# Expert numbers as bytes instead of four-byte integers in a routed mixture-of-experts kernel

## The reference

```python
idx = jnp.argmax(router_probs, axis=-1)
onehot = jax.nn.one_hot(idx, E, dtype=xt.dtype)
...
h = jnp.einsum('te,td,edf->tf', onehot, xn, W1) + b1[idx]
h = jax.nn.relu(h)
y = jnp.einsum('te,tf,efd->td', onehot, h, W2) + b2[idx]
y = y * gates
```

## Time and profile before

| | |
|---|---|
| median of three runs | 201.38 us |
| the profiled execution's own time | 202.25 us |
| its span | 200.5 us |
| mean granted clock of TensorE | 0.91 |
| PE busy | 147.8 us, 74% |
| DVE busy | 161.1 us, 80% |
| ACT busy | 148.1 us, 74% |
| POOL busy | 114.3 us, 57% |

### The profile page before, as it was taken

One profiled execution on the slowest core, in us unless ns is written; L12 is line 12 of the kernel. 1 busy time (PEld: TensorE's weight loads), 2 busy tenths in 40 slices (PEclk: granted clock), 3 DMA queues, 4 the chain that ended last, 5 costly groups with the idle time before them and its releaser, 6 DMA issues.

```text
span 200.5 us, 5489 instructions
## 1 busy us (share of the span) xinstructions
PE 147.8 (74%) x1446; PEld 118.1 (59%) x1446; DVE 161.1 (80%) x819; ACT 148.1 (74%) x448; POOL 114.3 (57%) x200
## 2 busy tenths in 40 slices
PE   0068979988997795922369878998998997999400
PEld 0015736857566474821316767987888996888200
DVE  2455287999998869699698899999999999799900
ACT  2358979997975696527645887999999999898520
POOL 4323140508789765634469215768677687578650
PEclk9999999999999998585556999999999999999955
DMA  5997184000101101101342212223222222110000
GB/s 131 346 394 261 26 273 159 3 0 15 40 26 35 42 29 41 54 15 40 77 126 83 56 30 55 66 71 76 65 75 64 66 64 69 53 54 19 28 9 0
DMA packets 16415, 15.74 MB, mean 79 GB/s; under 512 B 2810, under 2 KB 13142, under 8 KB 16386
## 3 DMA queue, kind: packets, MB, share of 16 engines
q1 hardware_dynamic: 14034, 11.10, 19.0%
q0 software_dynamic: 2272, 4.27, 6.4%
q10 hardware_dynamic: 80, 0.03, 0.1%
HBM read 10.52 MB, written 5.33 MB: 79 GB/s over the span
## 4 chain that ended last, share of the span: by engine, by line
PE 43%; DVE 33%; issue 8%; ACT 6%; DMA 3%; ACTq 2%; POOLq 1%; SPq 1%; POOL 0%; DVEq 0%
PE bank L473 7%; DVE hl L1239 6%; PE bank L592 6%; PE bank L430 5%; PE bank L445 4%; DMA XN<-in_attn_embeddings 3%; DVE z L1248 3%; PE bank L502 3%; PE bank L580 3%; PE bank L576 2%; PE bank L578 2%; DVE zpart L1244 2%; PE bank L579 2%; PE bank L595 2%; DVE bn L1252 2%
## 5 line engine op out<-in xcount | busy, mean ns | idle before, releaser
L418 POOL DMA_INDIRECT out<-OUT,tok x39 | 40.5, 1039 | 26.5 <-issue 25.0
L383 POOL DMA_INDIRECT rows<-R,place x32 | 31.8, 994 | 18.0 <-DVE place L919 9.4
L592 PE MATMUL bank<-W2hl,hh 128*128 x156 | 32.6, 274 | 7.0 <-issue 3.2
L576 PE MATMUL bank<-sel,bias 96*128 96x128 bf16 x156 | 34.6, 222 | 0.0
L578 PE MATMUL bank<-xh,W1h 128*128 128x128 f16 x156 | 34.2, 219 | 0.0
L580 PE MATMUL bank<-xh,W1l 128*128 128x128 f16 x156 | 34.1, 218 | 0.0
L579 PE MATMUL bank<-xl,W1h 128*128 128x128 f16 x156 | 34.0, 218 | 0.0
L1239 DVE SCALAR_TENSOR_TENSOR hl<-bank,hh 128x512 f16<-128x512 f32 x39 | 26.9, 690 | 3.5 <-ACT hh L746 2.6
L595 PE MATMUL bank<-W2hl,hl 128*128 x156 | 27.9, 219 | 0.0
L746 ACT ACTIVATE hh<-bank 128x512 f16<-128x512 f32 x39 | 23.1, 593 | 6.1 <-PE bank L580 5.8
L359 POOL TENSOR_TENSOR rmag<-guarded,minus_half 128x4 f32<-128x4 f32 x8 | 8.2, 1022 | 27.0 <-ACT guarded L615 27.0
(11 more groups left out here) (197 smaller groups left out, 459.3 us busy)
## 6 DMA issues: line engine op xcount, KB each, us to landing
XR<-rows SPq DMA_DIRECT2D x39, 66.0 KB
W<-in_ffn_W SPq DMA_DIRECT2D x1, 2048.0 KB, 11.0
X<-in_attn_embeddings SPq DMA_DIRECT2D x2, 512.0 KB, 8.6
X<-in_attn_embeddings SPq DMA_DIRECT2D x1, 768.0 KB
out<-OUT,tok POOLq DMA_INDIRECT x39
rows<-padt SPq DMA_DIRECT2D x9, 66.0 KB
XN<-in_attn_embeddings SPq DMA_DIRECT2D x2, 256.0 KB, 7.9
rows<-R,place POOLq DMA_INDIRECT x32
```

Of the source, the lines that this page charges most:

```text
L383: pool.indirect_dma_start(out=rows[:, :], out_offset=bass.IndirectOffsetOnAxis(ap=place[u][:, k:k + 1], axis=0), in_=R[u][:, k, :], in_off ...
L418: pool.indirect_dma_start(out=out[:, :], out_offset=bass.IndirectOffsetOnAxis(ap=tok[k][:, 0:1], axis=0), in_=OUT[k][:, :], in_offset=None ...
L576: pe.matmul(h, bias3[:, c * P:(c + 1) * P], sel, start=True, stop=False)
L592: pe.matmul(y[:, 0:2 * D], hh[k][:, c * P:(c + 1) * P], w, start=c == 0, stop=False)
```

## The change

The tile `blk_e` holds unsigned bytes instead of 32-bit integers. It has 48 places instead of 40, 48 bytes a partition instead of 160. DVE's two copies into it (L1139, L1184) now convert to bytes, and the five register loads of PE (L554) read bytes, still eight registers each and seven in the last. `blk_row` and `pad_row`, which SP reads, stay as they are. No instruction is added, removed or moved on any engine. In SBUF the tiles that are laid out behind `blk_e` stand 96 bytes lower.

```diff
-        blk_e = sb("blk_e", [P, 4 * (-(-NB // 4))], I32)
+        blk_e = sb("blk_e", [P, 16 * (-(-NB // 16))], mybir.dt.uint8)
```

## The result

The changed kernel takes 206.01 us (median of six runs, 204.99 to 206.91), against 201.39 us for the kernel before in the same comparison (six runs, 199.98 to 201.86). The ratio is 1.025, with a 95% interval of 1.021 to 1.029: slower by 2.5%. The forecast was 205.9 us, with a range of 200.7 to 207.8.

The account below looks back on a forecast made before the run. PE's register loads were taken to be on the path in the block stage, with DVE full. Terms 1.27 + 0 + 2.54 + 0.65 = 4.46 us took 201.38 to 205.8, and 0.1 for the clock made 205.9; range 200.7 to 207.8.

Parts of the forecast that it names:

- The bound: Block stage: a PE register load delays first matmul, `hh` and `hl`; DVE, full at 1.88 us a block, never regains it.
- The choice of eight single reads: PE's loads: eight bytes go one by one, 1.96 us a load, 1.27 more than the 689 ns mean; chance 0.57.
- The row with seven numbers: PE's last load, 1087 ns: its last three numbers, twelve bytes standing together, still cost three reads; taken to decide for single reads.
- The price of a read: PE's loads: a fixed part of 0.24 us plus 0.215 us for each separate read.
- Third and fourth load: PE's loads at 136.1 and 151.8 us: cover of 0.23 to 0.33 us used up, + 1.27 us each, 2.54 together.
- Fifth load: PE's load of seven at 167.2 us: four reads become seven, nothing left to hide in, + 0.65 us.
- First load: PE's load at 102.9 us: moves `xl`, the fillers and DVE's work behind them, + 1.27 us, at most 0.1 hidden.
- the 0.1 that I gave to the clock: TensorE's clock rise near 109 us may come later with the fillers; 0.1 us of it put into the forecast.
- Second load: PE's load at 119.0 us: hidden while DVE works through the second table, costed at 0; 1.0 us without that cover.
- Copies and placement: DVE's two byte copies, - 0.05 to + 0.05 us each, and tiles moved by 96 bytes, 1 us at most; both taken as 0.
- The range of the single reads: Whole kernel if eight bytes are eight single reads: 204.4 to 207.8 us, around 205.9.
- the clock's 1.7 us: Upper end of the 0 to 1.7 us put for a later rise of TensorE's clock behind the first load.

Follow-up runs that it names:

- the halfwords: Against the kernel before: 16-bit integers in blk_e, every load eight numbers, the last too; 206.85 us against 200.86, ratio 1.027.
- the sixteen bytes: Against the kernel before: bytes, sixteen numbers a load, then seven in step 28, with 32 registers; 211.26 us against 200.86, ratio 1.046.
- the second profile of before: The kernel before profiled again with no edit; one run, 201.69 us (before in its comparison: 200.86).
- the load of 24: Against the kernel before: integers, sixteen in one load in PE's first-half wait, the second table's 24 in one load in step 5; 203.14 us against 202.49, ratio 0.997.

## Why the prediction was right, point by point

The bound. That a register load of PE's sequencer is on the path and DVE's full stream makes every loss final held: behind the third, fourth and fifth load no time comes back, and in the table no stretch without a load moved by more than 0.13 us.

The choice of eight single reads. Right, but the rule that I drew for it was not the one that holds. The row with seven numbers gave the reads away. The argument was that less than sixteen bytes go singly; the halfwords and the sixteen bytes show that sixteen whole bytes of a smaller type go singly too, so of the types tried it is the four-byte one that is joined. For eight bytes both rules say the same, which is luck.

The price of a read. At eight reads the sum of the two parts was right, and the parts were not. I had 0.24 us fixed and 0.215 a read on PE. Sixteen bytes against eight give 0.245 a byte, and four integers in one read take 0.336 to 0.341, which leaves 0.10 fixed. By 0.10 + 0.24 a read, seven integers are 1.06 (measured 1.09 to 1.13), eight bytes 2.02 (1.93 to 2.06 behind the first load), seven bytes 1.78 (1.76 to 1.82), sixteen 3.94 (3.89), 24 integers 1.54 (1.63). Eight integers come out at 0.58, measured 0.61 to 0.75. Sixteen integers come out at 1.06, measured 1.29; they were the first load of their program, which in the other kernels is longer than a later one of its size (see the first load below). At eight reads my parts and these meet (1.96 and 2.02), which is luck.

Third and fourth load, + 1.27 each. Measured + 1.10 and + 1.34 against the first profile, + 1.26 and + 1.25 against the second. What a load can hide was put at 0.23 to 0.33 us; with bytes it is 1.93 - 1.49 = 0.44 and 2.02 - 1.54 = 0.48. I forecast 1.76 and 1.6 us of idle time and it is 1.49 and 1.54.

Fifth load, + 0.65. Against the second profile of before + 0.65, against the first + 0.03, because that one had a late matmul in the same step that I took for part of the load's cost. As four of the five profiles with seven integers have it, + 0.03 is the more common value, and that all the growth of this load is lost rests on one profile of before.

First load, + 1.27. This was the term that was too small. The load grew by 1.60 us, from 0.777 to 2.378, and is 0.44 longer than the next one. `xl` of block 0 starts at 106.96, where I had 106.7. The stretch from the load's start to `hl` of block 0 grew by 2.09 against the first profile of before and by 1.56 against the second, in which the clock rises 1.5 us later. The first profile is the unusual one: in the four others with integers in this load the stretch takes 8.17 to 8.20 us, and in the four with eight bytes or halfwords 9.47 to 9.77, so 1.3 to 1.6 more. Two executions of one kernel thus differ by 0.5 us here, and the 0.1 that I gave to the clock can't be told from that. By itself this load cost 2.1 us (1.0 to 3.2). Why the first load is longer than the others is not shown: in integers 0.78 against 0.61, in sixteen bytes 4.47 against 3.89, and SP's first of eight too, 0.72 to 0.74 against 0.49 to 0.53.

Second load, 0. In the changed kernel 0: `hl` of blocks 4 and 6 stand 4.57 us apart before and 4.58 after. I had `hh` done some 0.5 us before DVE wants it; it was 0.18. Alone the load cost 1.0 us (0.3 to 1.7) by the time, of which its profile shows 0.47 and puts it down to a late matmul. The step holds for the changed kernel and not for every kernel with this load.

Copies and placement, 0. The copy takes 173 ns (170 before), the reads of `XR` 385 to 430, and the bytes with all tiles in place are as slow.

The sum was 4.46 us. The span grew by 4.3 against the first profile of before and by 5.0 against the second, of which 0.3 lies ahead of the first load; the medians differ by 4.6. That the sum comes so near is partly luck. Against the first profile the first load is 0.8 over its term and the fifth 0.6 under it, and the two cancel. Against the second the fifth is as forecast and the sum is 0.2 to 0.5 short, most of it the first load's.

The range of the single reads. I gave 204.4 to 207.8 for reads of 150 to 250 ns and the clock's 1.7 us. With the same two sizes of a read for all terms, 3 x 6 x 0.15 + 3 x 0.15 = 3.15 and 5.25 us, it is 204.5 to 208.3. The measured time lies well inside either.

## What to carry to other kernels

A register load on the path is paid by the read, so keep its numbers as four-byte integers, load them in whole fours, and round the last load up instead of trimming it (eight integers took 0.72 us where seven took 1.10). Smaller data is not faster to read where the price is by the access. Where the engine has a little room in every step, several short loads that each fit into it leave less idle time than one long load (none, against 1.09 us behind the load of 24); and a stall of a sequencer is best looked for on the engine that has no slack, in its idle time, not in the busy shares.

## What the runs showed of the hardware

Register loads of PE from SBUF: four four-byte integers take 0.34 us, eight 0.61 to 0.75, seven 1.09 to 1.13, sixteen 1.29, 24 1.63; bytes and halfwords cost a read each, 1.76 to 1.82 us for seven bytes, 1.92 to 2.06 for eight of either, 3.89 for sixteen bytes. The first load of the program is longer: 0.78 for eight integers, 2.36 to 2.38 for eight bytes or halfwords, 4.47 for sixteen bytes. Four integers on SP take 0.30 to 0.31, but for one record of 21 ns in the first profile of before.

The Trainium skill, Runtime: NRT & Kernel Launch, section Instruction fetch mechanics, has about 200 ns for each register, and its page describes such loads as coming from HBM, not from SBUF. For bytes and halfwords the rows here have some 245 ns each, of the same size; for integers in whole fours they disagree, with 84 ns for each of four. The Trainium skill, DMA: Bandwidth & Descriptors, section Latency and other measured facts, has a floor of some 600 ns without saying for which memory. The rows undercut it, on SP with 303 ns and on PE with 336.

Not expected and not explained: in some executions the first matmul of a block behind a load is done 0.5 to 0.6 us later than its records and the usual 0.3 us say, that of block 30 in four profiles and that of block 6 in one. The second profile of before does not have it.
